# A fused attention and feed-forward layer on one core: which engine's queue issues a head's weights and the row of reciprocals

## The reference

```python
h = layernorm(x)
q = (h @ Wq_c.T + bq_c) @ Wq_up.T + bq_up          # 32 heads of 192
kv_nope, kv_rope = split(h @ Wkv_c.T + bkv_c)      # 64 + 64
k, v = up(kv_nope), kv_rope shared by all heads
x = x + sum_over_heads(softmax(q k.T / sqrt(192)) v) @ Wo.T + bo
x = x + ffn(layernorm(x))                          # three layers of +1/-1 weights
```

## Time and profile before

| what | us |
|---|---|
| median of 3 runs (1936.48 to 1956.7) | 1937.24 |
| the profiled execution's own time | 1945.14 |
| its span, first to last instruction | 1943.3 |
| busy: PE / DVE / ACT / POOL | 1578.4 / 1578.7 / 1395.2 / 1067.6 |

### The profile page before, as it was taken

The page is one execution under the profiler, slowest core; times in us unless marked ns, Lnnn a source line. Parts: engine busy times, 40 slices in busy tenths (PEclk is TensorE's granted clock), DMA queues, the critical chain, the costliest instruction groups (busy, mean ns, idle before and its releaser), DMA issues. The chain is left out here.

```text
span 1943.3 us, 22707 instructions
## 1 busy us (share of the span) xinstructions
PE 1578.4 (81%) x7060; PEld 712.9 (37%) x7060; DVE 1578.7 (81%) x1960; ACT 1395.2 (72%) x1979; POOL 1067.6 (55%) x1228
## 2 busy tenths in 40 slices
PE   7878878788778878788878888878878888788799
PEld 6633333333333333333333333333333333333244
DVE  6588888888878878888878888888888888888575
ACT  5587777778767767877767877777777777787422
POOL 3346555656546656665645565566555656565420
PEclk9999999999999999999989999999999999999799
DMA  6599999999999999999999999999999999999801
GB/s 203 202 193 199 199 187 187 198 186 203 191 179 197 186 194 200 203 194 192 203 171 195 191 197 203 198 205 197 203 188 188 204 201 203 196 202 193 179 33 64
DMA packets 1139346, 364.62 MB, mean 188 GB/s; under 512 B 1090816, under 2 KB 1113376, under 8 KB 1139232
## 3 DMA queue, kind: packets, MB, share of 16 engines
q1 hardware_dynamic: 1135136, 354.83, 98.0%
q0 software_dynamic: 4096, 8.40, 2.4%
HBM read 83.95 MB, written 10.75 MB: 49 GB/s over the span
## 5 line engine op out<-in xcount | busy, mean ns | idle before, releaser
L958 DVE TENSOR_REDUCE mx<-S 128x1 f32<-128x1024 f32 x512 | 623.0, 1217 | 236.1 <-PE S L833 235.9
L913 ACT ACTIVATE S<-S,shift,unscale 128x1024 f32<-128x1024 f32 x512 | 601.8, 1175 | 123.7 <-DVE shift L964 123.2
L950 DVE TENSOR_TENSOR halves<-S,halves 128x1024 f16<-128x1024 f32 x512 | 622.8, 1216 | 29.2 <-ACT halves L922 27.3
L831 PE MATMUL S<-kvTH,qeH 128*128 128x512 f16 x1024 | 402.2, 393 | 264.5 <-POOL qeL L756 139.3
L922 ACT ACTIVATE halves<-S 128x1024 f16<-128x1024 f32 x512 | 523.9, 1023 | 40.8 <-DMA PT<-halves 25.6
L785 POOL TENSOR_TENSOR onormH<-osum,recip_row 128x512 fp32r<-128x512 f32 x127 | 194.2, 1529 | 520.1 <-DMA recip_row<-row_scratch 440.7
L833 PE MATMUL S<-kvTH,qeL 128*128 128x512 f16 x1024 | 398.0, 389 | 0.0
L832 PE MATMUL S<-kvTL,qeH 128*128 128x512 f16 x1024 | 397.7, 388 | 0.0
L831 PEld LDWEIGHTS S<-kvTH,qeH 128*128 128x128 f16 x1024 | 100.4, 98 | 533.9 <-POOL qeL L756 195.0
L929 ACT ACTIVATE osum<-O 128x512 f32<-128x512 f32 x128 | 76.4, 597 | 264.5 <-PE O L846 264.4
L964 DVE SCALAR_TENSOR_TENSOR shift<-mx,unscale,c_lift 128x1 f32<-128x1 f32 x512 | 243.7, 476 | 18.1
(11 more groups left out here) (256 smaller groups left out, 1713.7 us busy)
## 6 DMA issues: line engine op xcount, KB each, us to landing
recip_row<-row_scratch SPq DMA_DIRECT2D x128, 256.0 KB, 4.3
weff<-weff_scratch SPq DMA_DIRECT2D x128, 192.0 KB, 3.1
wv<-in_wv POOLq DMA_DIRECT2D x128, 64.0 KB, 4.3
PT<-halves SPq DMA_TRANSPOSE x512, 4.9
raw<-in_raw SPq DMA_DIRECT2D x8, 772.0 KB, 5.5
weff_scratch<-w_split SPq DMA_DIRECT2D x8, 768.0 KB, 5.2
x<-in_x SPq DMA_DIRECT2D x4, 1024.0 KB, 7.1
x_all<-in_x SPq DMA_DIRECT2D x3, 1024.0 KB, 5.5
```

Source lines behind the costliest of these rows:

```text
L831: mm(out, qeH[par][:, q], keep["kvTH"][:, keys], start=True, stop=False)
L913: nc.scalar.activation(S[:, t % SLOTS, :], S[:, t % SLOTS, :], ACT.Exp, bias=shift[:, col:col + 1], scale=keep["unscale"][:, 0:1], accum_o ...
L950: v.tensor_tensor(halves[u][:, 1, :], S[:, t % SLOTS, :], halves[u][:, 0, :], ALU.subtract).then_inc(low_out, 1)
L958: v.reduce_max(mx[:, col:col + 1], S[:, t % SLOTS, :], AX.X).then_inc(max_ready, 1)
```

## The change

SP keeps the transposes alone. POOL issues the load of `weff` (`load_weights`), the store of the row (`store_row`) and its load (`load_row`). POOL's step is put in a new order: issue `wv`; L785 and L786; issue the store; L790; `split_q`; issue `weff`; issue the row's load (after a wait for the store's landing); L774, L775, L777; `ahead`. The weights of steps 0 and 1 are still loaded by SP in `prepare`; for later steps PE waits on new semaphores `weff_next`.

```diff
@@ -631,6 +631,7 @@
         wv_in = [sem(f"wv_in{i}") for i in range(2)]
         row_in = keep["row_in"]
         turned = [sem(f"turned{i}") for i in range(UN)]
+        weff_next = [sem(f"weff_next{i}") for i in range(2)]
         names = ("bv_in", "ones_set", "scores_ready", "max_ready", "shift_ready", "probs_ready",
                  "high_out", "low_out", "recip_ready", "recip_out", "pv_done", "onorm_ready", "wv_done", "vsum_out",
                  "wv_split", "onorm_high", "onorm_low", "ffn_in", "row_ready", "bo_added", "projected0", "summed0",
@@ -663,11 +664,6 @@
 
         @block.sync
         def _(sp):
-            def load(g, weights, par):
-
-                sp.wait_ge(q_filled, g - 1)
-                sp.dma_start(f32(weff[par][:].rearrange("p t c -> p (t c)")), weights).then_inc(weff_in[par], 16)
-
             sp.dma_start(bv[:], dram["bv"]).then_inc(bv_in, 16)
 
             sp.dma_start(keep["x0"][:], dram["x"][0:BLK, :].rearrange("(t p) d -> p t d", p=P)).then_inc(ffn_in, 16)
@@ -684,26 +680,13 @@
                              transpose=True).then_inc(turned[u], 16)
 
             def body(g, b, h, par):
-                last = 1 - par
-                if exists(g + 2):
-                    load(g + 2, dram["weff_h"][(h + 2) % NH], par)
-                if exists(g - 1):
-
-                    sp.wait_ge(recip_ready, g)
-                    sp.dma_start(dram["row"][last].rearrange("(p u) -> p u", u=UN),
-                                 recip[:, last * UN:(last + 1) * UN]).then_inc(recip_out, 16)
                 if exists(g):
                     if g >= 2:
                         sp.wait_ge(pv_done, g - 1)
-                    turn(g, 0, par)
-                if exists(g - 1):
-                    sp.wait_ge(recip_out, 16 * g)
-                    sp.dma_start(recip_row[last][:], dram["row"][last].partition_broadcast(P)).then_inc(row_in[last], 16)
-                if exists(g):
-                    for u in range(1, UN):
+                    for u in range(UN):
                         turn(g, u, par)
 
-            steps(sp, body, after=1)
+            steps(sp, body, after=0)
 
         @block.gpsimd
         def _(pool):
@@ -757,24 +740,25 @@
 
             split_q(0, 0)
 
+            def load_weights(g, weights, par):
+                pool.wait_ge(q_filled, g - 1)
+                pool.dma_start(f32(weff[par][:].rearrange("p t c -> p (t c)")), weights).then_inc(weff_next[par], 16)
+
+            def store_row(g, i):
+
+                pool.wait_ge(recip_ready, g + 1)
+                pool.dma_start(dram["row"][i].rearrange("(p u) -> p u", u=UN),
+                               recip[:, i * UN:(i + 1) * UN]).then_inc(recip_out, 16)
+
+            def load_row(g, i):
+                pool.wait_ge(recip_out, 16 * (g + 1))
+                pool.dma_start(recip_row[i][:], dram["row"][i].partition_broadcast(P)).then_inc(row_in[i], 16)
+
             def body(g, b, h, par):
                 if exists(g):
                     if g >= 2:
                         pool.wait_ge(wv_split, g - 1)
                     pool.dma_start(wv[par][:], dram["wv"][h]).then_inc(wv_in[par], 16)
-                if g in ahead:
-                    pool.wait_ge(ffn_in, 16 * 9)
-                    pool.wait_ge(q_low, g + 1)
-                    ahead[g]()
-                if exists(g - 1):
-                    i = 1 - par
-                    if g >= 3:
-                        pool.wait_ge(wv_done, g - 2)
-                    pool.wait_ge(wv_in[i], 16 * turns(g - 1, i))
-                    nc.gpsimd.tensor_tensor(wvH[i][:], wv[i][:], unit[:], ALU.mult).then_inc(copied, 1)
-                    nc.gpsimd.tensor_tensor(wvs[:], wv[i][0:KVL, :], unit[0:KVL, :], ALU.mult).then_inc(copied, 1)
-                    pool.wait_ge(copied, 2 * g)
-                    nc.gpsimd.tensor_tensor(wvL[i][:], wvs[:], f32(wvH[i][0:KVL, :]), ALU.subtract).then_inc(wv_split, 1)
                 if exists(g - 2) and exists(g - 1):
                     pool.wait_ge(row_in[par], 16 * turns(g - 2, par))
                     pool.wait_ge(o_out, g - 1)
@@ -785,11 +769,29 @@
                     nc.gpsimd.tensor_tensor(in_order(onormH[:]), in_order(osum[:]), row, ALU.mult).then_inc(onorm_high, 1)
                     nc.gpsimd.tensor_tensor(in_order(onorm[:]), in_order(osum[0:KVL, :]), row[0:KVL],
                                             ALU.mult).then_inc(onorm_ready, 1)
+                if exists(g - 1):
+                    store_row(g - 1, 1 - par)
+                if exists(g - 2) and exists(g - 1):
                     pool.wait_ge(onorm_high, g - 1)
                     pool.wait_ge(onorm_ready, g - 1)
                     nc.gpsimd.tensor_tensor(onormL[:], onorm[:], f32(onormH[0:KVL, :]), ALU.subtract).then_inc(onorm_low, 1)
                 if exists(g) and exists(g + 1):
                     split_q(g + 1, 1 - par)
+                if exists(g + 2):
+                    load_weights(g + 2, dram["weff_h"][(h + 2) % NH], par)
+                if exists(g - 1):
+                    i = 1 - par
+                    load_row(g - 1, i)
+                    if g >= 3:
+                        pool.wait_ge(wv_done, g - 2)
+                    pool.wait_ge(wv_in[i], 16 * turns(g - 1, i))
+                    nc.gpsimd.tensor_tensor(wvH[i][:], wv[i][:], unit[:], ALU.mult).then_inc(copied, 1)
+                    nc.gpsimd.tensor_tensor(wvs[:], wv[i][0:KVL, :], unit[0:KVL, :], ALU.mult).then_inc(copied, 1)
+                    pool.wait_ge(copied, 2 * g)
+                    nc.gpsimd.tensor_tensor(wvL[i][:], wvs[:], f32(wvH[i][0:KVL, :]), ALU.subtract).then_inc(wv_split, 1)
+                if g in ahead:
+                    pool.wait_ge(ffn_in, 16 * 9)
+                    ahead[g]()
 
             steps(pool, body)
 
@@ -799,7 +801,10 @@
 
             def project_queries(nxt, b, i):
 
-                pe.wait_ge(weff_in[i], 16 * turns(nxt, i))
+                if nxt < 2:
+                    pe.wait_ge(weff_in[i], 16)
+                else:
+                    pe.wait_ge(weff_next[i], 16 * (nxt // 2))
                 tok = slice(b * BLK, (b + 1) * BLK)
                 w = weff[i]
                 mm(O[:], w[:, 0, :], keep["qaH"][:, tok], start=True, stop=False)
```

## The result

| | before | changed |
|---|---|---|
| median of 4 runs each, same chip | 1939.28 us (1936.48 to 1956.70) | 1996.72 us (1980.02 to 2005.34) |
| profiled execution, span | 1945.14, 1943.3 us | 2004.17, 2002.3 us |
| mean granted clock of TensorE | 0.973 | 0.939 |

The ratio is 1.0266, 95% interval 1.0168 to 1.0365. The forecast was 1900, so even the sign was wrong. Most of the parts that it was summed from can be found in the new trace at their forecast size. The loss stands in a quantity for which the sum had no term.

A forecast was written before the change was run, and what follows sets the result against it. It took POOL's chain behind the row's arrival, delayed by SP's queue, as the bound. Row-limited start 6.0 plus chain with store 7.0 gave 13.0 us against 13.30, 37 us off over 124 steps: 1900 us, range 1845 to 1987.

The forecast's parts named there:

- w: Time in the step at which POOL issues the row's load; put at 0.6 to 0.8 us, 0.6 used.
- s: Start of POOL's L785, counted from the step's first score; forecast at 6.0 us, range 5.5 to 6.3.
- s + 8.1: Step length when L785 starts before about 5.35 us and DVE's shift of tile 1 is caught by L786.
- s + 6.4 + c: Step length through POOL's chain from L785 to the next scores, with the store's issue added; s + 7.0.
- c: Issue time of the row's store on POOL, between L786 and L790; taken as 0.6 us, bounds 0.3 to 1.2.
- step 122: Profiled step of 12.1 us before the change: row a little later, s = 5.48, shift escaping between L785 and L786.
- 6.0 + 7.0 = 13.0 us a step against 13.30, for 124 steps: Forecast's sum: L785's start plus POOL's chain with the store, 0.30 us saved a step, 37 us in all.
- step 61: Profiled step of 14.33 us before the change: late row, s = 7.81, clock fallen after PE's idle stretch.
- Late row: Rival, chance 0.27: the row lands after 6.4 us on POOL's queue, steps take 14.0 us, total 2024 us.
- s + 7.0 for all steps: Step length with the store on POOL's chain, claimed from s = 5.5 on; 14.0 us at s = 7.0.
- Early row: Rival, chance 0.13: the row lands before osum, every shift is caught, steps take 13.1 to 13.35 us, total 1925.
- Full DMA engines: Rival, chance 0.12: the DMA engines set the step, which stays at 13.30 us, total 1937 us.

The follow-up runs named there:

- e3: Changed kernel with the row's load issued ahead of the weights' load on POOL; 1971.26 us, ratio 1.020.
- e8: Changed kernel with the weights issued by SyncE again, POOL keeping both transfers of the row; 1949.97 us, ratio 1.008.
- e1: Changed kernel with the row's store issued earlier, before POOL's first product (L785 of before); 1926.59 us, ratio 0.998.
- e13: Changed kernel with the weights issued by SyncE and three unread TensorE matmuls behind the output; 1947.94 us, ratio 1.005.
- e9: Changed kernel with the store ahead of the first product and two idle GpSimd products in front of onormL; 2026.16 us, ratio 1.051.
- e6: Changed kernel with the store ahead of the first product and three unread TensorE matmuls behind the output; 1930.92 us, ratio 0.996.
- e14: Changed kernel with the store ahead of the first product and the weights issued by SyncE, no unread matmuls; 1935.05 us, ratio 1.001.

## Why the prediction was wrong

**What held.** The row was issued at w = 0.43 (0.6 taken), landed 5.4 us after it (5.4 taken), and s was 5.8 in the median and 6.0 on average in the untouched steps (6.0 taken). The store's issue was 0.58 (0.6). `weff` on POOL was waited for 8.5 us in all, 8 times, and its issue and the row's are done before `osum`. The rule s + 8.1 held, in the changed kernel's bad steps and in e3 and e8. Untouched steps took 12.73 us, less than the 13.0 of the sum.

**An over-sized term that did no harm.** The store's issue "is added to POOL's chain: s + 6.4 + c". That chain measured 6.69 from L769 to the next scores. The kernel before has 6.56 there in its steps with s over 5.4 (median of 28), and so has e1. So c counted 0.13 us and not 0.6: ACT's `qef` comes so late that POOL would have waited for it anyway. The 6.4 was 0.16 too low: at step 122 the 6.64 that the trace has was lowered to 6.3 by the wait for ACT. By the same token the issue looked harmless. The delay that it causes is not on POOL's chain at all but on the branch that leaves it at `onormL`, toward TensorE's output.

**The step that failed** is the sum, "6.0 + 7.0 = 13.0 us a step against 13.30, for 124 steps". It takes every step at the full clock, and so has no term for falls: the price of the store on TensorE's side stood at nothing, and no reason was given for it. The comparison is uneven too, as the 13.30 is a mean that has the falls of before in it. With before's share (29 of 121) the changed kernel's step would be 0.24 x 14.72 + 0.76 x 12.73 = 13.2. Before's own by the same reckoning, with 14.28 and 13.06, is 13.35, so 17 us would be left of the 37. With its own, 56 of 120 or 0.47, it is 13.7, which is 0.3 us a step slower than before instead of 0.3 faster. The forecast did see the clock, at step 61 and in the early stretch of the earlier trace rows with 0.95, but only as a thing that a late row does. Nothing asked what the 0.6 us in front of `onormL` do to TensorE: they lengthen its stretch by only 0.12 us, from 2.52 to 2.64, and 24 falls stand behind stretches of that length. A look at who waits for L790, `PE V L859`, would have led there: in the list of waits it grew from 61.9 to 113.6 us.

**The rivals.** Late row came nearest in time (2024) and has a part in it: 28 rows landed after 7 us, 26 of them more than 6.6 us after their issue, and no row of the kernel before took that long. Whether that is because `weff` goes first, as it said, the runs do not settle (e1 against e13). But before had 28 late rows too, and in 28 of the 34 touched steps without a late row the row was there before `osum`. Its sign, L785 "past 6.5 with steps over 13.5 and a clock below 1.00", is met by steps in which `osum` is late and not the row; the sign was too coarse to tell the two apart. Its price, s + 7.0 for all steps, was not paid. Early row is the state of e3 and e8, and their untouched steps took the 13.1 that it gave. Full DMA engines are ruled out: the share is 1.06 in steps of 12.5 us and 0.88 in those of 14.7.

**How the loss divides.** In the profiled executions the steps from 3 to 126 take 44 us more (1718 against 1674 us). By kinds: untouched steps with no late row stand 25 us better, touched ones with no late row 52 us worse, steps with late rows 13 us worse and the three that close a block 4. (Each number is the kind's excess over 12.9 us a step, after less before.) The remaining 15 us are ahead of and behind these steps, where the changed kernel's profile has four falls more. 11 of them are ahead of step 3: step 2 alone, whose row lands 11.8 us into it, takes 18.7 us instead of 13.0.

**What stays open.** Why about half of the 2.6 us stretches bring a fall and half do not; what makes rows land late, and single ones only after 9 to 11 us; why the shift once slips between two instructions of POOL and in e9 waits for five; and why e6, e13 and e14, with 10 to 12 falls fewer than before, stand at 0.996 to 1.005 of it. For the last, e13 and e14 show caught shifts in the place of falls (tile 1's shift took over 1.05 us in 92 and 80 of their 121 steps, in the kernel before in 70), but no run removed both. e6 has 43 of them, and there it is open: its profiled execution, 1916.73 us, is the fastest of its ten. No fill made a kernel clearly faster. That the falls cost the time rests on e1, on the way from slow matmuls to a late `osum` in the bad step above, and on the lengths of touched and untouched steps.

## What to carry to other kernels

- A change that trims the critical engine also moves the branches that leave its chain. Follow the branch to TensorE and sum what it idles between two runs of matmuls. Here the store's 0.58 us on GpSimd made that stretch only 0.12 us longer, and nearly every second step took 14.7 us instead of 12.7, though the chain that I had computed was as forecast or shorter.
- Split the steps by granted clock before you average, and forecast both the length of an undisturbed step and the share of disturbed ones. A mean over both hides a term.
- Issue a small DMA in front of an instruction that has to wait anyway, not between two that are needed: with the same store the kernel stood at 1.027 to 1.031 of before in the one place, and at 0.998 in the other.

## What the runs showed of the hardware

- TensorE's granted clock fell behind 76 of 170 stretches of 2.56 to 2.70 us and behind 1 of 696 of 2.40 to 2.56, though both hold the same three output matmuls. The waits around these were 0.93 and 0.75 us in the changed kernel, and 0.51 and 1.05 in e1, which had no such fall. In kernels with three unread matmuls in the stretch it was 0 of 145.
- A VectorE instruction of 0.22 us took 4.10 us behind five GpSimd instructions in a row, 16 times in one run (e9). It was never held for more than 2.3 us in the changed kernel, whose products have the store's issue between them, nor for more than 1.7 us in the kernel before, which has three products in a row.
- Two loads on GpSimd's queue: the 256 KB issued behind the 192 KB took more than 6.6 us to land 26 times of 121 in the changed kernel and 11 times in e1; with the 192 KB on SyncE's queue, 10 times in e8 and 19 in e13. The median landing hardly moved, 5.4 us in the changed kernel against 5.1 in e8. The place of the 192 KB does not settle it.
